# A two-layer attention and feed-forward block on one core: in the second attention layer the transpositions of q and k stand one step earlier

## The chip, the cores and the metric

The kernel runs on one core of a Trainium2 chip. The time is the device time of one execution of the whole program in microseconds (us); the median of several runs counts. The core has five engines that run their own instruction streams and wait for one another through semaphores: TensorE (PE, matmuls; PEld is its weight load), VectorE (DVE), ScalarE (ACT), GpSimd (POOL) and SyncE (SP), which only issues DMAs here.

## The reference

The input x is 2 x 512 tokens of 512 numbers in fp32. Four sublayers follow one another, each as x + layernorm(sublayer(layernorm(x))): a causal attention with rotary positions and grouped heads, a linear layer with LoRA, a second attention, and a SwiGLU feed-forward with LoRA. The change touches the second attention alone:

```python
q = (hidden_states @ Wq + bq).reshape(b, n, H, HD)      # H = 32 heads of HD = 128
k = (hidden_states @ Wk + bk).reshape(b, n, H, HD)
v = (hidden_states @ Wv + bv).reshape(b, n, H, HD)
q = rmsnorm(q, gq)
k = rmsnorm(k, gk)
scores = jnp.einsum('bnhd,bmhd->bhnm', q, k) * scale
attn = jax.nn.softmax(scores.astype(jnp.float32), axis=-1).astype(q.dtype)
out = jnp.einsum('bhnm,bmhd->bnhd', attn, v).reshape(b, n, H * HD)
return out @ Wo + bo
```

## The kernel before

Every fp32 product is made of three matmuls of halves (`product`, L83 to L85): hi x lo, lo x hi, hi x hi. Whatever enters a product is therefore split in two: ACT copies it into the rounded `_hi`, and DVE or POOL makes the remainder `_lo`.

The second attention is `paired_attention`. Its 32 heads are worked in NG = 8 groups of 4; group 0 and group 7 are written out, groups 1 to 6 are the six rounds of a hardware loop (`passes`, L252). A group has 8 **slots**, each one head of one of the two sequences, and 32 **steps** n = 0 to 31, four to a slot: step 4s + t makes the scores of slot s for 128 queries t against all 512 keys. Two slots of the same sequence form a pair (r, b). On each step every engine runs the same scheme for its own part:

- PE: the scores of step n (`l_score`, three matmuls of 128x512), and behind them what the table `USES1` has due at n: for a pair four tiles `y` (q and k of two heads for 128 tokens, 12 matmuls), two `v` (24 matmuls of 128x256), and for each slot one transposition of q (`tq`, four 128x128 transpositions at L485), one of k (`tk`), and the product of probabilities and v (`pv`, 12 matmuls that take the four chunks k = 0 to 3 of the transposed probabilities in turn). Output products (`l_out`) stand last in a step.
- DVE: negated row maximum of step n (`tops`, L675), the block transposition of the probabilities of step n - 1 (`turn_blocks`, L690), and then, one step behind PE, what empties the banks that PE filled: `l_y` (L639), `l_qT_lo` (L90), `l_kT_lo` (L646), `l_v_lo` (L90), `l_scaled` (L652, after `pv`). `l_probsT_lo` of the odd chunks and the additions to `acc` follow.
- ACT: exponentials of step n (L573), then, one step behind PE, `l_qT_hi` (L553), `l_kT_hi` (L555) or `l_v_hi` (L551), then `l_probsT_hi` (L579, two chunks at steps 4s + 8 and two at 4s + 9), squares of `y` for the RMS norm (L566), and the rounding of weights (L543).
- POOL: `l_probsT_lo` of the even chunks, the RMS norm (L748, L753), the remainders of weights (all L90).
- SP: the 16 DMAs that carry the block-transposed probabilities of a slot into `l_moved`, at step 4s + 4.

The table sets the order. An entry's number is the PE step, reckoned from the first step of the group; entries below zero belong to the group before. Inside one step the rank is y, v, tq, tk, pv. All uses share the four PSUM banks `general` in one ring: a use waits until the use four places ahead of it has been emptied (`n = m.done(USES1, x, d) - len(general)`, L459). `Pass.turns` gives each engine its due entries, DVE and ACT with a lag of one.

The waits around the change: the first scores of a slot wait until DVE has emptied the bank of `tk`, that is for `l_kT_lo` (L521), and all scores wait for the exponentials two steps back (L522). A `tq` of a pair's first slot waits for the pair's normed `y` (`s_yn`, L482). DVE writes a pair's first `y` only once the `tk` that still reads the old `y` is done.

```python
USES1 = {("y", r, b, t): 16 * r + 8 * b + n for r, b in PAIRS for t, n in enumerate((-15, -13, -12, -11))}
USES1 |= {("v", r, b, u): 16 * r + 8 * b + 7 + u for r, b in PAIRS for u in range(2)}
```

Of the kernel before, what the change touches and what calls it, by code (L numbers as in the profile page):

```python
# [33 lines left out]
SLOTS = GH * B  # L34
# [225 lines left out]
TURN_AT, MOVE_AT, LAND_AT, PV_AT, REST_AT = 1, 4, 8, 10, 12  # L260
# [12 lines left out]
PAIRS = [(r, b) for r in range(2) for b in range(B)]  # L273
USES1 = {("y", r, b, t): 16 * r + 8 * b + n for r, b in PAIRS for t, n in enumerate((-15, -13, -12, -11))}
USES1 |= {("v", r, b, u): 16 * r + 8 * b + 7 + u for r, b in PAIRS for u in range(2)}
USES1 |= {(kind, s): 4 * s + n for kind, n in (("tq", -3), ("tk", -2), ("pv", PV_AT)) for s in range(SLOTS)}
USES1 = Plan(USES1, lambda x: ("y", "v", "tq", "tk", "pv").index(x[0]))
OUTS1 = Plan({(r, b, t): 16 * r + 8 * b + 17 + t // 2 for r, b in PAIRS for t in range(TB)}, lambda x: x)
LOADS1 = {("wqk", r, c): 16 * r - 22 + c for r in range(2) for c in range(C)}
# [1697 lines left out]
```

How the kernel before makes its waits and increments, by code:

```python
def wait_past(engine, sem, m, per, count):  # L60
    if m.first and not (isinstance(count, int) and count > 0):
        return
    engine.wait_ge(sem, m.i * per + count)
# [70 lines left out]
    def spread(self, dve, *tiles):  # L135
        for r, t in tiles:
            dve.wait_ge(self.measured[r], 3 * t + 1)
            dve.bn_aggr(self.mean_var[:, r, t], self.stats[:, r, t]).then_inc(self.measured[r], 1)
        for r, t in tiles:
            dve.wait_ge(self.measured[r], 3 * t + 2)
            dve.tensor_scalar(self.var[:, r, t:t + 1], self.mean_var[:, r, t, 1:2], LN_EPS, None, ALU.add)\
                .then_inc(self.measured[r], 1)
# [1 line left out]
    def root(self, pool, r, t):  # L145
        pool.wait_ge(self.measured[r], 3 * t + 3)
        pool.tensor_tensor(self.rstd[:, r, t:t + 1], self.var[:, r, t:t + 1], self.half[:, 0:1], ALU.pow)\
            .then_inc(self.rooted[r], 1)
# [1 line left out]
    def center(self, dve, r, t):  # L151
        dve.wait_ge(self.rooted[r], t + 1)
        dve.scalar_tensor_tensor(self.bias[:, r, t:t + 1], self.mean_var[:, r, t, 0:1], -1.0,
                                 self.rstd[:, r, t:t + 1], ALU.mult, ALU.mult).then_inc(self.biased[r], 1)
# [1 line left out]
    def scaled(self, act, r, t, out, rows):  # L157
        act.wait_ge(self.biased[r], t + 1)
        act.activation(out, rows, ACT.Identity, bias=self.bias[:, r, t:t + 1], scale=self.rstd[:, r, t:t + 1])\
            .then_inc(self.normed[r], 1)
# [812 lines left out]
        @block.tensor  # L974
# [37 lines left out]
            for t in range(TT):
                pe.wait_ge(norms.normed[0], t + 1)
                if t >= 2:
```

## Time and profile before

| | us |
|---|---|
| median of 3 runs | 2364.04 (2362.09 to 2365.25) |
| the profiled execution, its own time | 2368.55 |
| its span, first to last instruction | 2366.8 |
| PE busy | 2132.5 (90%) |
| DVE busy | 1659.9 (70%) |
| ACT busy | 1296.0 (55%) |
| POOL busy | 1197.0 (51%) |

All views below are of this profiled execution. The second attention runs from 896 to 2109 us of the span. A view by instruction shows the start, the duration, the engine, the line, and the tiles as out<-in; the bracket is the idle time of the engine just before, and what ended it.

### The profile page before, as it was taken

The page shows a single profiled execution, that of the slowest core. Times are in us where ns is not written, and L with a number is a line of the kernel's source. Part 1 is how long each engine was busy: PE and PEld are TensorE (multiplying, and loading weights), DVE is VectorE, ACT ScalarE, POOL GpSimd, SP SyncE. Part 2 cuts the span into 40 slices and gives each one's busy share as a digit, 9 for nine tenths or more (in the row PEclk, how much of TensorE's full clock was granted, in tenths as well). Part 3 has the DMA queues.
Part 4 walks back from the last instruction along what each step waited for, and adds up shares of the span by engine and source line. Part 5 has one row for each costly group of instructions (what it writes and reads, how often), then busy time and mean ns, then how long its engine had stood idle before and what let it go on. Part 6 is the DMA issues. An engine that isn't in the chain of part 4 may idle for free. (4 is left out here: it accounts for less than half of the span.)

```text
span 2366.8 us, 38519 instructions
## 1 busy us (share of the span) xinstructions
PE 2132.5 (90%) x10535; PEld 1774.2 (75%) x10535; DVE 1659.9 (70%) x3013; ACT 1296.0 (55%) x3541; POOL 1197.0 (51%) x960
## 2 busy tenths in 40 slices
PE   4899999999999546999999999999999999756998
PEld 3688788888878435788878888788888888645887
DVE  3777777777778552777877878777778887754422
ACT  3666666666665343665655656656656566424321
POOL 4776766777664244544545445455454553324310
PEclk9999999999999777999999999999999999976999
DMA  2444343434434211444434344344444343333210
GB/s 72 109 111 112 107 114 106 118 94 115 119 85 118 88 62 33 115 113 108 105 89 117 103 111 106 91 113 107 111 107 105 93 112 89 94 116 99 77 45 27
DMA packets 165877, 231.51 MB, mean 98 GB/s; under 512 B 47281, under 2 KB 77137, under 8 KB 165745
## 3 DMA queue, kind: packets, MB, share of 16 engines
q1 hardware_dynamic: 165744, 229.97, 36.2%
q8 instruction: 56, 0.92, 0.2%
q14 instruction: 77, 0.62, 0.1%
HBM read 114.23 MB, written 6.55 MB: 51 GB/s over the span
## 5 line engine op out<-in xcount | busy, mean ns | idle before, releaser
L90 POOL TENSOR_TENSOR l_probsT_lo<-l_moved,l_probsT_hi 128x512 fp32r<-128x512 f32 (+2 forms) x256 | 289.6, 1136 | 274.0 <-ACT l_probsT_hi L579 247.1
L573 ACT ACTIVATE l_probs<-l_score,l_negtop 128x512 f32<-128x512 f32 x256 | 175.1, 684 | 342.8 <-DVE l_negtop L675 332.2
L90 DVE TENSOR_TENSOR l_probsT_lo<-l_moved,l_probsT_hi 128x512 fp32r<-128x512 f32 (+1 forms) x256 | 282.1, 1102 | 53.8 <-ACT l_probsT_hi L579 49.3
L1105 ACT ACTIVATE l_probs<-l_score,l_negtop 128x128 f32<-128x128 f32 (+3 forms) x256 | 134.9, 527 | 252.2 <-DVE l_negtop L1198 250.4
L83 PE MATMUL l_score<-l_kT_lo,l_qT_hi 128*128 128x512 f32 (+3 forms) x512 | 192.2, 375 | 55.8 <-DVE l_kT_lo L646 31.5
L83 PE MATMUL l_general<-l_w_qk_lo,xT_hi 128*128 128x512 f32 x512 | 201.7, 394 | 27.9 <-POOL l_w_qk_lo L90 27.9
L83 PE MATMUL l_out<-l_w_out_lo,l_oT_hi 128*128 128x512 f32 x512 | 209.2, 409 | 3.8 <-DVE l_oT_lo L701 2.8
L83 PE MATMUL l_general<-l_probsT_lo,l_v_hi 128*128 128x512 f32 (+3 forms) x512 | 189.2, 369 | 23.7 <-POOL l_probsT_lo L90 11.7
L675 DVE TENSOR_REDUCE l_negtop<-l_score 128x1 f32<-128x512 f32 x256 | 175.1, 684 | 40.4 <-PE l_score L85 37.5
L84 PE MATMUL l_general<-l_w_qk_hi,xT_lo 128*128 128x512 f32 x512 | 201.1, 393 | 0.0
L85 PE MATMUL l_general<-l_w_qk_hi,xT_hi 128*128 128x512 f32 x512 | 201.1, 393 | 0.0
L85 PE MATMUL l_out<-l_w_out_hi,l_oT_hi 128*128 128x512 f32 x512 | 201.0, 393 | 0.0
L84 PE MATMUL l_out<-l_w_out_hi,l_oT_lo 128*128 128x512 f32 x512 | 201.0, 393 | 0.0
L1198 DVE CUSTOM_DVE_ANT_0 l_score<-l_score,l_mask 128x128 f32<-128x128 f32 (+3 forms) x256 | 126.2, 493 | 88.4 <-PE l_score L85 88.0
L85 PE MATMUL l_general<-l_probsT_hi,l_v_hi 128*128 128x512 f32 (+3 forms) x512 | 184.9, 361 | 0.0
L84 PE MATMUL l_general<-l_probsT_hi,l_v_lo 128*128 128x512 f32 (+3 forms) x512 | 184.4, 360 | 0.0
L84 PE MATMUL l_score<-l_kT_hi,l_qT_lo 128*128 128x512 f32 (+3 forms) x512 | 184.1, 360 | 0.0
L85 PE MATMUL l_score<-l_kT_hi,l_qT_hi 128*128 128x512 f32 (+3 forms) x512 | 184.1, 360 | 0.0
L690 DVE STREAM_TRANSPOSE l_blocks<-l_probs 128x512 f32<-128x512 f32 x256 | 177.6, 694 | 0.2 <-ACT l_probs L573 0.2
L566 ACT ACTIVATE l_squares<-l_y 128x128 f32<-128x128 f32 x512 | 151.9, 298 | 40.2 <-DVE l_y L639 37.8
L83 PEld LDWEIGHTS l_score<-l_kT_lo,l_qT_hi 128*128 128x128 f32 x512 | 96.8, 189 | 101.2 <-issue 39.6
L90 POOL TENSOR_TENSOR l_w_qk_lo<-l_raw_qk,l_w_qk_hi 128x512 fp32r<-128x512 f32 x64 | 82.2, 1289 | 178.3 <-ACT l_w_qk_hi L543 178.3
(198 smaller groups left out, 6252.2 us busy)
## 6 DMA issues: line engine op xcount, KB each, us to landing
l_moved<-l_blocks SPq DMA_DIRECT2D x1024, 64.0 KB, 2.0
l_moved<-l_blocks SPq DMA_DIRECT2D x512, 80.0 KB, 2.1
l_inv_all<-inv_rows SPq DMA_DIRECT2D x32, 512.0 KB, 4.2
l_raw_out<-l_wo SPq DMA_DIRECT2D x64, 256.0 KB, 4.1
l_inv_all<-inv_rows SPq DMA_DIRECT2D x64, 256.0 KB, 3.6
ffn_w_lo_words<-f_w SPq DMA_DIRECT2D x33, 256.0 KB, 2.8
l_raw_q<-l_wq SPq DMA_DIRECT2D x32, 256.0 KB, 4.2
l_raw_qk<-l_wq SPq DMA_DIRECT2D x64, 128.0 KB, 2.9
```

The costliest lines, as they stand in the source:

```text
L83: nc.tensor.matmul(out, left.hi, right.lo, start=first, stop=False, skip_group_check=True)
L84: nc.tensor.matmul(out, left.lo, right.hi, start=False, stop=False, skip_group_check=True)
L85: return nc.tensor.matmul(out, left.hi, right.hi, start=False, stop=last, skip_group_check=True)
L90: return engine.tensor_tensor(out, full, hi.bitcast(F32), ALU.subtract)
L566: last = act.activation(squares[:, h], y[:, b, t, h * HD:(h + 1) * HD], ACT.Square, accum_out=sumsq[:, b, j:j + 1])
L573: act.activation(probs[:, n % NPR], score[n % 2][:], ACT.Exp, bias=negtop[:, n:n + 1], accum_out=total[:, n:n + 1]).then_inc(s_exp, 1)
L675: dve.tensor_reduce(negtop[:, n:n + 1], score[n % 2][:], AXX, ALU.max, negate=True)\
L690: dve.transpose(to, probs[:, n % NPR]).then_inc(s_block, 1)
L1105: act.activation(probs[:, n % NPR, 0:width[t]], score[n % 2][:, 0:width[t]], ACT.Exp, bias=negtop[:, n:n + 1], scale=-1.0, accum_out=total ...
L1198: dve.tensor_tensor_reduce(out=score[n % 2][:, 0:w], in0=score[n % 2][:, 0:w], in1=mask[:, S - w:S], scale=-SCALE, scalar=3.0e38, op0=ALU. ...
```

## The change

One tuple of `USES1` is altered. `tq` goes from step 4s - 3 to 4s - 4, and `tk` from 4s - 2 to 4s - 3. No instruction is added or taken away; the bank numbers follow the new order.

```diff
-USES1 |= {(kind, s): 4 * s + n for kind, n in (("tq", -3), ("tk", -2), ("pv", PV_AT)) for s in range(SLOTS)}
+USES1 |= {(kind, s): 4 * s + n for kind, n in (("tq", -4), ("tk", -3), ("pv", PV_AT)) for s in range(SLOTS)}
```

What this does to the order of work is seen at three places. The first is DVE in the loop body, steps 14 and 15, ahead of the scores of slot 4 (step 16); L675 opens a step. Before:

```order
1023 L675 TENSOR_REDUCE l1_negtop<-l1_score0 128x1
1024 L690 STREAM_TRANSPOSE l1_blocks<-l1_probs 128x4x4x32
1025 L630 REGISTER_ALU
1026 L639 TENSOR_TENSOR l1_y<-l1_general2,l1_b_qk 128x512
1027 L628 REGISTER_ALU
1028 L90 TENSOR_TENSOR l1_qT_lo<-l1_general3,l1_qT_hi 128x512
1029 L674 REGISTER_ALU
1030 L675 TENSOR_REDUCE l1_negtop<-l1_score1 128x1
1031 L690 STREAM_TRANSPOSE l1_blocks<-l1_probs 128x4x4x32
1032 L628 REGISTER_ALU
1033 L646 SCALAR_TENSOR_TENSOR l1_kT_lo<-l1_general0,l1_gains,l1_kT_hi 128x512
```

and now:

```order
1025 L675 TENSOR_REDUCE l1_negtop<-l1_score0 128x1
1026 L690 STREAM_TRANSPOSE l1_blocks<-l1_probs 128x4x4x32
1027 L630 REGISTER_ALU
1028 L639 TENSOR_TENSOR l1_y<-l1_general3,l1_b_qk 128x512
1029 L628 REGISTER_ALU
1030 L646 SCALAR_TENSOR_TENSOR l1_kT_lo<-l1_general0,l1_gains,l1_kT_hi 128x512
1031 L674 REGISTER_ALU
1032 L675 TENSOR_REDUCE l1_negtop<-l1_score1 128x1
1033 L690 STREAM_TRANSPOSE l1_blocks<-l1_probs 128x4x4x32
```

`l1_kT_lo` has moved from step 15, the last before the scores that need it, to step 14; `l1_qT_lo` has moved from step 14 to step 13.

The second is ACT in the loop body at step 13, where the chunks 2 and 3 of the transposed probabilities are rounded that `pv` takes at step 14; L573 opens the step. Before:

```order
682 L573 ACTIVATE l1_probs,l1_total<-l1_score1,l1_negtop 128x512
683 L579 ACTIVATE l1_probsT_hi<-l1_moved 128x4x128 x2
684 L559 REGISTER_ALU
685 L563 REGISTER_ALU
686 L566 ACTIVATE l1_squares,l1_sumsq<-l1_y 128x128 x4
```

and now:

```order
683 L573 ACTIVATE l1_probs,l1_total<-l1_score1,l1_negtop 128x512
684 L548 REGISTER_ALU
685 L553 ACTIVATE l1_qT_hi<-l1_general2 128x512
686 L579 ACTIVATE l1_probsT_hi<-l1_moved 128x4x128 x2
687 L559 REGISTER_ALU
688 L563 REGISTER_ALU
689 L566 ACTIVATE l1_squares,l1_sumsq<-l1_y 128x128 x4
```

`l1_qT_hi` now stands between the exponentials and `l1_probsT_hi`.

The third is PE in group 7, where no `y` stands between the uses: steps 21 and 22, up to the first chunk of `pv`. L485 are the transpositions. Before:

```order
3510 L83 MATMUL l1_score1<-l1_kT_lo,l1_qT_hi 128x512
3511 L84 MATMUL l1_score1<-l1_kT_hi,l1_qT_lo 128x512
3512 L85 MATMUL l1_score1<-l1_kT_hi,l1_qT_hi 128x512
3513 L485 MATMUL l1_general3<-ident,l1_y 128x128
3514 L485 MATMUL l1_general3<-ident,l1_y 128x128 x3
3515 L83 MATMUL l1_score0<-l1_kT_lo,l1_qT_hi 128x512
3516 L84 MATMUL l1_score0<-l1_kT_hi,l1_qT_lo 128x512
3517 L85 MATMUL l1_score0<-l1_kT_hi,l1_qT_hi 128x512
3518 L485 MATMUL l1_general0<-ident,l1_y 128x128
3519 L485 MATMUL l1_general0<-ident,l1_y 128x128 x3
3520 L83 MATMUL l1_general1<-l1_probsT_lo,l1_v_hi 128x512
```

and now:

```order
3510 L485 MATMUL l1_general3<-ident,l1_y 128x128
3511 L485 MATMUL l1_general3<-ident,l1_y 128x128 x3
3512 L83 MATMUL l1_score1<-l1_kT_lo,l1_qT_hi 128x512
3513 L84 MATMUL l1_score1<-l1_kT_hi,l1_qT_lo 128x512
3514 L85 MATMUL l1_score1<-l1_kT_hi,l1_qT_hi 128x512
3515 L485 MATMUL l1_general0<-ident,l1_y 128x128
3516 L485 MATMUL l1_general0<-ident,l1_y 128x128 x3
3517 L83 MATMUL l1_score0<-l1_kT_lo,l1_qT_hi 128x512
3518 L84 MATMUL l1_score0<-l1_kT_hi,l1_qT_lo 128x512
3519 L85 MATMUL l1_score0<-l1_kT_hi,l1_qT_hi 128x512
3520 L83 MATMUL l1_general1<-l1_probsT_lo,l1_v_hi 128x512
```

Both transpositions have passed one set of scores; `pv` follows its step's scores directly.

At the opening of the layer, which runs ahead of group 0, the order of PE's uses was y of pair (0,1) tiles 0 to 3, tq, tk. It is now y tiles 0 to 2, tq, y tile 3, tk.

## Rows read from the trace of the kernel before

**Rows 1.** The page: busy time, share of the span, instructions of each engine.

```profile
PE 2132.5 (90%) x10535; PEld 1774.2 (75%) x10535; DVE 1659.9 (70%) x3013; ACT 1296.0 (55%) x3541; POOL 1197.0 (51%) x960
```

**Rows 2.** Busy time by stretch: PE, PEld, DVE, ACT, POOL; then granted clock, DMA, GB/s.

```profile
1212.80:1216.20 3.40, 3.40 (x18) 3.40 (x17) 3.40 (x6) 2.30 (x5) 3.32 (x4) 0.50 0.19 41
1216.00:2026.00 810.00, 791.60 (x4107) 665.65 (x4105) 641.45 (x925) 482.00 (x1500) 401.21 (x286) 1.00 0.41 104
```

**Rows 3.** PE's waits from 896 to 2109: us in total, times, longest.

```profile
PE l_score L83 <- DVE l_kT_lo L646: 31.5, 59, 3.1
...
PE l_score L83 <- issue: 2.6, 1, 2.6
PE l_score L83 <- DVE l_scaled L652: 2.4, 1, 2.4
```

**Rows 4.** Instructions in order of time: the first scores of an odd slot.

```profile
1376.79 0.68 ACT L555 ACTIVATE l_kT_hi<-l_general,l_gains 128x512 fp32r<-128x512 f32 x1
...
1377.50 0.75 DVE L646 SCALAR_TENSOR_TENSOR l_kT_lo<-l_general,l_gains,l_kT_hi 128x512 fp32r<-128x512 f32 x1 [0.81 <-ACT l_kT_hi L555]
1377.67 0.39 PE L85 MATMUL l_general<-l_w_qk_hi,xT_hi 128*128 128x512 f32 x1
...
1378.38 0.49 PE L83 MATMUL l_score<-l_kT_lo,l_qT_hi 128*128 128x512 f32 x1 [0.32 <-DVE l_kT_lo L646]
...
1378.71 0.39 PE L84 MATMUL l_score<-l_kT_hi,l_qT_lo 128*128 128x512 f32 x1
```

**Rows 5.** The same wait at an ordinary turn of the loop, slot 0.

```profile
1648.77 0.49 PE L83 MATMUL l_score<-l_kT_lo,l_qT_hi 128*128 128x512 f32 x1 [0.71 <-DVE l_kT_lo L646]
```

**Rows 6.** Slot 0 at two turns of the loop.

```profile
1211.42 0.49 PE L83 MATMUL l_score<-l_kT_lo,l_qT_hi 128*128 128x512 f32 x1 [2.62 <-issue]
...
1501.42 0.75 DVE L646 SCALAR_TENSOR_TENSOR l_kT_lo<-l_general,l_gains,l_kT_hi 128x512 fp32r<-128x512 f32 x1 [1.19 <-ACT l_kT_hi L555]
...
1504.04 0.49 PE L83 MATMUL l_score<-l_kT_lo,l_qT_hi 128*128 128x512 f32 x1 [2.44 <-DVE l_scaled L652]
```

**Rows 7.** Steps 13 and 14 of a loop round: chunks 2 and 3 of slot 1.

```profile
1421.45 1.14 ACT L579 ACTIVATE l_probsT_hi<-l_moved 128x512 fp32r<-128x512 f32 x2
...
1422.21 1.28 POOL L90 TENSOR_TENSOR l_probsT_lo<-l_moved,l_probsT_hi 128x512 fp32r<-128x512 f32 x1
...
1422.36 0.60 PE L485 MATMUL l_general<-ident,l_y 128*128 128x128 f32 x4
...
1422.62 1.43 DVE L90 TENSOR_TENSOR l_probsT_lo<-l_moved,l_probsT_hi 128x512 fp32r<-128x512 f32 x1 [0.81 <-ACT l_probsT_hi L579]
...
1424.19 0.39 PE L83 MATMUL l_general<-l_probsT_lo,l_v_hi 128*128 128x512 f32 x1
...
1424.88 0.39 PE L83 MATMUL l_general<-l_probsT_lo,l_v_hi 128*128 128x512 f32 x1
```

**Rows 8.** Chunk 2 of slot 0 in the same round.

```profile
1403.20 1.75 POOL L90 TENSOR_TENSOR l_probsT_lo<-l_moved,l_probsT_hi 128x512 fp32r<-128x512 f32 x1
...
1406.32 0.39 PE L83 MATMUL l_general<-l_probsT_lo,l_v_hi 128*128 128x512 f32 x1
```

**Rows 9.** The opening: norm of pair (0,0), y tile 2 emptied, transpositions, first scores.

```profile
915.56 4.04 POOL L753 TENSOR_TENSOR l_y<-l_y,l_meansq 128x512 f32<-128x512 f32 x4
...
918.38 0.69 DVE L639 TENSOR_TENSOR l_y<-l_general,l_b_qk 128x512 f32<-128x512 f32 x1 [2.03 <-PE l_general L85]
...
925.08 0.50 PE L83 MATMUL l_score<-l_kT_lo,l_qT_hi 128*128 128x512 f32 x1 [3.14 <-DVE l_kT_lo L646]
```

**Rows 10.** Group 7, steps 19 and 20, on DVE and PE.

```profile
2026.86 0.70 DVE L690 STREAM_TRANSPOSE l_blocks<-l_probs 128x512 f32<-128x512 f32 x1
...
2029.03 1.06 DVE L652 TENSOR_TENSOR l_scaled<-l_general,l_inv_all 128x512 f32<-128x512 f32 x1
2029.17 0.80 PE L83 MATMUL l_score<-l_kT_lo,l_qT_hi 128*128 128x512 f32 x1 [2.96 <-DVE l_kT_lo L646]
...
2030.86 0.69 DVE L675 TENSOR_REDUCE l_negtop<-l_score 128x1 f32<-128x512 f32 x1 [0.77 <-PE l_score L85]
```

## The prediction

> **What bounds the kernel now.** The page says that PE is busy 90% of the span and the other engines 51 to 70% [rows 1]. That is a mean over all layers, so the next view is the busy time of the stretch that the change touches: from 1216 to 2026 us of the second attention PE is busy 791.6 of 810.0 us, at the full clock (granted 1.00, the 2.4 GHz level), DVE 79%, ACT 60%, POOL 50% [rows 2]. PE is the bound there, and a step can be gained only where PE stands still. The list of PE's waits says where: the largest is `l_score` at L83 on DVE's `l_kT_lo`, 31.5 us in 59 waits; two more of the same place are put down to other names, 2.6 and 2.4 us [rows 3]. They are two first scores of a group at a turn of the loop [rows 6]. That makes 36.5 us in 61 waits, close to one for each of the 64 slots: nearly every slot begins with PE waiting for k.
>
> The instructions in time order show why. At step 4s - 1 ACT does its exponentials, then `l_kT_hi` (1376.79 to 1377.47), then DVE makes `l_kT_lo` (1377.50 to 1378.25, after 0.81 us idle), and 0.13 us after its end the scores start [rows 4]. PE had been done 0.32 us earlier. The chain hangs on the exponentials of the step just before, not on the transposition, which PE made a step ahead.
>
> **Part 1: the wait goes.** `l_kT_lo` moves one step ahead on DVE and `l_kT_hi` on ACT, 3.5 us and more before the scores; the wait is at most 0.7 us at ordinary places [rows 5]. What does one wait cost in full? Normally a matmul of this shape starts 0.23 us after the one before (two chunks of `pv`, three matmuls apart, start 0.69 apart [rows 7]). The last matmul ahead of the scores starts at 1377.67, the scores at 1378.38: 0.71 us, of which 0.23 is normal, so 0.48 where 0.32 is booked as idle; and from there to L84 it takes 0.33, 0.10 more than normal [rows 4]. Each wait costs its idle time and 0.26 us. Over 61 waits: 36.5 + 61 x 0.26 = 52.4 us.
>
> **What of it stays.** (a) The first wait of the layer, 3.14 us [rows 9], hangs on its own transposition and has no step to hide behind: 3.4 with the 0.26. (b) The two turns of the loop with 2.62 and 2.44 us. At the second `l_kT_lo` ended at 1502.17 and the scores began at 1504.04, 1.87 later where 0.13 is usual [rows 4, 6]: something else was late by 1.7, and by 1.9 at the other (2.62 less the 0.71 of an ordinary turn [rows 5, 6]). I keep both: 3.6. (c) The opening. PE now wants `tq` after y tile 2, which it had finished by 918.38, but the norm of that pair ends at 915.56 + 4.04 = 919.60 [rows 9]: 1.3 us of new waiting, which POOL passes on to the next weights. The wait of slot 1, 2.0 us in the sum, is eaten by that 1.3 and by weights that come no sooner: 2.0. (d) In group 7 PE has little else to do, and DVE's chain counts. At step 20 the scores waited 2.96 us and the maxima began at 2030.86; without `l_kT_lo` DVE would go from the transposition (ends 2027.56) to `l_scaled` (1.06) and be at the maxima by 2028.6 [rows 10]. Of 3.2 us (with the 0.26) 2.2 are won and 1.0 stays; slot 7, at step 28, has the same order of work and I take the same: 2.0. The sum is 52.4 - 3.4 - 3.6 - 2.0 - 2.0 = **41.4 us**.
>
> **Part 2: what is moved past what.** No instruction is added. ACT does `l_qT_hi` at steps 4s - 3, just ahead of `l_probsT_hi` of chunks 2 and 3, and DVE `l_qT_lo` ahead of `l_probsT_lo` of chunk 3; `pv` of the slot before wants these one PE step on. This is the place where a new wait could arise. In a loop round, slot 1: POOL ends chunk 2 at 1423.49 and PE takes it at 1424.19, 0.70 later; DVE ends chunk 3 at 1424.05 and PE takes it at 1424.88, 0.83 later [rows 7]. Slot 0 has 1.37 [rows 8]. PE's `pv` comes sooner by one block of transpositions, 0.60 at most [rows 7]. ACT's `l_qT_hi` has no row of its own; the nearest is `l_kT_hi`, 0.68, and for `l_qT_lo` it is `l_kT_lo`, 0.75 [rows 4]. From above: all in series, chunk 3 comes 0.68 + 0.75 + 0.13 later and is wanted 0.60 sooner, 2.2 less the 0.83 is 1.3 us in slots 1 and 5, 16 times: 21 us. From below nothing, since both engines also lose work ahead of it: at the end of the step before the slot DVE drops 0.81 of waiting and 0.75 of `l_kT_lo`, so `l_scaled` and all behind it run up to 1.5 us sooner, and PE only 0.5. I take nothing, nearer the lower end, because steps 4s to 4s + 2 form one chain on ACT and DVE, and that chain starts sooner by more than is put into it.
>
> The ring of four banks: at steps 1 and 5 of 8 `tk` now comes one use nearer to its predecessor, but the use four ahead was emptied by DVE in the step before, and a whole `y` (12 x 0.23 = 2.7 us on PE) stands between. Nothing. POOL and SP keep their order. The exponentials that the scores wait for lie two steps back, and their order is not touched.
>
> The order of ports. DVE's chunk 3 takes 1.43 us while POOL is at work beside it [rows 7]. The Trainium skill (SBUF — State Buffer, Who interferes with whom) says that a DVE instruction with two SBUF inputs and a GpSimd instruction that reads SBUF shut each other out for a whole instruction; by it a chunk 3 that slips behind POOL's next instruction would wait for all of it. With 1.3 us for that, 16 times, its sum would be as high as the 21 us above; the rows agree that the two stretch when side by side, and do not show which slips.
>
> The turns of the loop. Of six, two show an extra 1.7 to 1.9 us [rows 6] and one ordinary one shows 0.71 [rows 5]. It may be that something at every turn takes up to 0.71 and now lies under the wait for k; bound 0 to 4 x 0.71 = 2.8 us. I take 0. The Trainium skill (Runtime: NRT & Kernel Launch, Instruction fetch mechanics) says that a taken branch whose target is not in the two pages held forces a fetch before the engine goes on; by it all turns would pay, and the sum would be 38.5.
>
> The clock. After the 2.62 us of idle the granted clock was 0.50 (1.2 GHz) from 1212.8 to 1216.2 [rows 2, 6]. If it stays full there, some 1.5 us more are won; not in the sum.
>
> **The time.** The profiled execution took 2368.55 us, 4.5 over the median of 2364.04; 41.4 off it would leave 2327.2, and off the median 2322.6. I forecast **2323**.
>
> **Rivals.** *A: the probabilities come late.* ACT and DVE don't make up for the moved pair, and chunks 2 and 3 bind in slots 1 and 5: 41 - 21 = 20 us won, 2344 at the worst, about 2340 with part of it. For it: the smallest margins of the layer, 0.70 and 0.83. Against it: the head start of 1.5 us.
> *B: slower.* The same place, but the shift grows along the chain, since DVE is 79% busy and its instructions stretch beside POOL. Per group the change wins about 5.1 us. If all eight `pv` come late by L against today's order, the loss per group is 2 (L - 0.70) + 6 (L - 1.37), which passes 5.1 at L = 1.84 us. At L = 2.2 it is 8.0, 2.9 a group more than is won, 8 groups: 23 us slower, 2387. For it: the moved pair together is 1.56 and the 0.60 of PE make 2.2. Against it: that takes everything in series and no head start anywhere.
> *C: a wait takes its place.* The scores start no sooner, since `tk` waits for its bank or `l_kT_lo` sits behind other work on DVE: 2364. Against it: `l_kT_lo` would have to come later by a whole step, 3.5 us.
> *D: more.* The two long turns and the clock go as well: 41.4 + 3.6 + 1.5 = 46.5, 2317.5; with small gains 2314.
>
> **How the numbers follow.** The forecast with its small terms (2314 to 2331) gets 0.74, D lies in it; A 0.16; C 0.05; B 0.05. The range must leave out no more than 0.2: from 2314 to 2342 it holds the forecast and most of A. A measurement of this kernel tells 0.2%, 4.7 us, from no change. Faster by more: 0.74 + 0.16 and nothing of C, 0.90; same 0.05; slower 0.05.
>
> **What would show it.** In the profile after: PE's waits of `l_score` on `l_kT_lo` gone but for the first, some 3 to 5 us left in all; PE busy over 99% from 1216 to about 1990; the layer shorter by about 41 us, each group of the loop by 5; `l_score` starting 3 us after `l_kT_lo` ends; about 1.3 us of PE idle before `tq` at 918. A shows as PE waits of `l_general` L83 on `l_probsT_lo`, 16 of about 1 us; B as the same in all slots; C as waits of `l_score` or L485 on DVE. Wrong would be the step that says ACT and DVE start sooner than they are loaded, or that the first scores wait for k alone.

## The result and the profile after

The changed kernel took 2334.53 us (median of 4 runs, 2332.97 to 2336.80) against 2363.51 us for the kernel before (4 runs, 2362.09 to 2365.25). The ratio is 0.9873, with a 95% interval of 0.9861 to 0.9886: faster by 29.0 us. The forecast was 2323, 41.4 us less, in a range from 2314 to 2342. The sign and the range held; of the forecast gain, 0.70 came. The profiled execution took 2333.02 us (span 2331.2) against 2368.55 us (span 2366.8), so the two traces differ by 35.6 us in the span.

The page's first line, which answers to [rows 1], and PE's waits from 896 to 2109 us, which answer to [rows 3] (us in total, times, longest):

```profile
PE 2118.4 (91%) x10535; PEld 1776.9 (76%) x10535; DVE 1643.7 (71%) x3013; ACT 1294.0 (56%) x3541; POOL 1181.9 (51%) x960
```

```profile
PE l_score L83 <- issue: 8.5, 5, 2.2
...
PE l_score L83 <- ACT l_probs L573: 4.0, 4, 1.3
PE l_score L83 <- DVE l_kT_lo L646: 3.1, 1, 3.1
...
PE l_general L485 <- POOL l_y L753: 1.4, 1, 1.4
```

Sixty of the 61 waits for k are gone; the one left is the first of the layer, 3.1 us. What is new is the first row: five waits of the first scores, 8.5 us in all, with nothing that the profile shows as their releaser ("issue"). The row on ACT belongs to the last group, that on POOL to the opening. The dots leave out other rows, among them PE's waits in `pv` for `l_probsT_lo`: 9.0 us in 5, all in and behind the last group, where the kernel before had 11.7 us in 6.

The first scores of an odd slot in the changed kernel, in order of time, as in [rows 4]:

```profile
1357.79 0.68 ACT L555 ACTIVATE l_kT_hi<-l_general,l_gains 128x512 fp32r<-128x512 f32 x1
...
1358.50 0.75 DVE L646 SCALAR_TENSOR_TENSOR l_kT_lo<-l_general,l_gains,l_kT_hi 128x512 fp32r<-128x512 f32 x1 [0.23 <-ACT l_kT_hi L555]
...
1365.02 0.39 PE L83 MATMUL l_score<-l_kT_lo,l_qT_hi 128*128 128x512 f32 x1
```

k is ready at 1359.25 and wanted at 1365.02, 5.77 us later; the scores carry no idle time. In even slots inside a round the margin is 2.7 us.

PE busy by stretch, at and behind the first turn of the loop, as in [rows 2] (us, busy of PE, PEld, DVE, ACT, POOL, granted clock, DMA, GB/s):

```profile
1201.30:1204.70 3.40, 3.40 (x13) 3.11 (x14) 1.73 (x4) 0.93 (x3) 3.32 (x4) 0.50 0.03 7
1205.00:1990.00 785.00, 778.25 (x4098) 665.32 (x4097) 629.44 (x923) 481.34 (x1501) 389.20 (x285) 1.00 0.42 107
```

PE is busy 99.1% of the loop's stretch. Of the 6.75 us that are left, 6.38 stand at the four turns of the loop in this stretch. One of them, with the last matmul ahead of it:

```profile
1342.32 0.28 PE L85 MATMUL l_general<-l_w_v_hi,xT_hi 128*128 128x256 f32 x1
...
1344.28 0.49 PE L83 MATMUL l_score<-l_kT_lo,l_qT_hi 128*128 128x512 f32 x1 [1.68 <-issue]
```

All five turns look like this, at 1201.28, 1344.28, 1486.19, 1627.44 and 1769.25 us, with 2.16, 1.68, 1.64, 1.41 and 1.65 us of idle PE. In the kernel before two of five were long [rows 6] and an ordinary one had 0.71 us, which was the wait for k [rows 5]. (Groups 1 to 6 are the loop, so it turns back five times; the "six" of the prediction was one too many.)

The span by stage, from the starts of PE's instructions at each border, in us. The forecast column is the prediction's own sum, cut at the same borders (idle time for k there, 0.26 more for each wait, less what was to stay):

| stage | before | after | gained | forecast |
|---|---|---|---|---|
| first y tile to the first scores, and group 0 | 168.5 | 162.9 | 5.6 | 4.5 |
| groups 1 to 6, the loop | 873.3 | 849.8 | 23.5 | 30.5 |
| group 7 to the last scores | 133.9 | 127.6 | 6.3 | 6.4 |
| end of the layer | 36.9 | 36.1 | 0.8 | 0 |
| sum | 1212.6 | 1176.4 | 36.2 | 41.4 |

The loop falls short by 7.0 us; the rest comes out 1.8 us above its forecast.

### The profile page after: what moved, and what is told of

Its sections match the earlier page's. It is cut to its first block and busy times, and to the rows that moved or that the text cites. A ratio compares the mean times of both kernels' runs of the same rounds, so it can differ in the third digit from the quotient of the medians.

```text
span 2331.2 us, 38519 instructions
## 1 busy us (share of the span) xinstructions
PE 2118.4 (91%) x10535; PEld 1776.9 (76%) x10535; DVE 1643.7 (71%) x3013; ACT 1294.0 (56%) x3541; POOL 1181.9 (51%) x960
## 5 line engine op out<-in xcount | busy, mean ns | idle before, releaser
L90 POOL TENSOR_TENSOR l_probsT_lo<-l_moved,l_probsT_hi 128x512 fp32r<-128x512 f32 (+2 forms) x256 | 272.1, 1068 | 309.8 <-ACT l_probsT_hi L579 282.8
L573 ACT ACTIVATE l_probs<-l_score,l_negtop 128x512 f32<-128x512 f32 x256 | 175.7, 686 | 381.2 <-DVE l_negtop L675 381.0
L675 DVE TENSOR_REDUCE l_negtop<-l_score 128x1 f32<-128x512 f32 x256 | 175.8, 687 | 99.7 <-PE l_score L85 97.6
L579 ACT ACTIVATE l_probsT_hi<-l_moved 128x512 fp32r<-128x512 f32 x256 | 147.1, 629 | 0.0
```

The lines of the kernel that those rows point to most:

```text
L90: return engine.tensor_tensor(out, full, hi.bitcast(F32), ALU.subtract)
L573: act.activation(probs[:, n % NPR], score[n % 2][:], ACT.Exp, bias=negtop[:, n:n + 1], accum_out=total[:, n:n + 1]).then_inc(s_exp, 1)
L579: act.activation(probsT_hi[:, :, k], moved[:, slot % 2, :, k], ACT.Copy).then_inc(s_land_hi, 1)
L675: dve.tensor_reduce(negtop[:, n:n + 1], score[n % 2][:], AXX, ALU.max, negate=True)\
```

## What the experiments asked

Two questions. Is it the place of k alone that makes the gain? And why are all five turns slow now, which the prediction had bounded at 2.8 us and set to nothing? The page of each kernel has a row on the instruction fetches: queue, packets, MB, share of the engines. That of the kernel before, and then that of the changed one:

```profile
q8 instruction: 56, 0.92, 0.2%
```

```profile
q8 instruction: 83, 1.36, 0.3%
```

Each of these packets has 16,384 bytes. In the compiled program an instruction of PE takes 64, so a packet carries 256; the run with 256 empty instructions below fetches just one packet more. PE's program in the changed kernel has 9,789 instructions, 38.2 packets. The body of the loop has 1,592 of them in both kernels, 4785 to 6376 counted from 0 (the traces record 1,590 in a round). Counted from the start of the program, it begins at instruction 178 of a packet and ends at 233 of the sixth packet after it, so it touches seven.

In the trace of the kernel before, no packet is fetched in the rounds that follow a quick turn, and nine in each of the two that follow a slow one; in the changed kernel nine are fetched in each of the five rounds (38 + 2 x 9 = 56, 38 + 5 x 9 = 83; a round is counted here from 2 us ahead of the branch that leads into it). The packets' times tie them to the stops. In the changed kernel the branch that ends a round is executed at 1196.92, 1340.40, 1482.35, 1623.83 and 1765.39 us. Each time one fetch starts 0.8 to 1.0 us ahead of it and another 1.0 us behind it, which takes 0.9 to 1.5 us, and then the first scores start. Both slow turns of the kernel before have the fetch 1.0 us behind the branch too; its three quick turns have none within 10 us.

All experiments are compared with runs of the kernel before that were taken beside them; its medians there were 2364.7, 2365.1 and 2366.0 us. The changed kernel itself was not run again beside them: its 2334.5 us is that of the first comparison.

## Experiments on the turns of the loop

**Written out.** The loop over groups becomes straight code, in both kernels.

```diff
+def written_out(engine, body, end):
+    for i in range(NG):
+        body(Pass(i, i == 0, i == NG - 1, end))
...
-            passes(pe, body, END1)
+            written_out(pe, body, END1)
```

(the same on SP, ACT, DVE and POOL)

> The changed kernel with the eight groups of the second attention written out, so that there is no loop and no turn in it. Theory 1 and theory 2 both: no idle at slot 0 of groups 2 to 6, 2334 less 10 to 12 = about 2323 us, if bringing in code in a row costs nothing, as groups 0 and 7 suggest. If code that comes in a row does cost, stalls appear in the middle of groups, and the time is not under 2330.

> The kernel before with the eight groups written out. The wait for k stays at every slot (0.17 to 0.71 us idle each); 2363.5 less 0 to 4 = about 2361 us. Against after_written_out it gives what the change is worth where no loop is in play: 38 to 42 us by the sum of the waits; 29 if the shortfall lies in the waits themselves and not in the turns.

The changed kernel written out took 2320.34 us (2318.45 to 2321.21), ratio 0.9811 [0.9795, 0.9827]; the kernel before written out 2359.96 us (2358.5 to 2360.94), ratio 0.9976 [0.9967, 0.9986]. Without turns the change is worth 39.6 us, within 2 us of the forecast 41.4 and inside the 38 to 42 that were expected. PE in the changed kernel written out, from 1210 to 1980:

```profile
1210.00:1980.00 770.00, 770.00 (x4061) 659.25 (x4060) 624.98 (x917) 476.54 (x1495) 383.00 (x282) 1.00 0.42 109
```

PE is never idle there, though 32 packets are fetched in this stretch (67 in the whole program). A fetch in straight code costs nothing that can be seen; a fetch at a turn does.

**Shift by 80.** The loop stays, and 80 empty instructions go ahead of PE's part of the layer, in both kernels.

```diff
+            for _ in range(80):
+                pe.wait_ge(s_const, 64)
+                pe.nop(nofuse=True)
             for x in USES1.early:
                 bank_use(x, start, 0)
```

> The changed kernel with 80 more instructions on PE, waits on a semaphore that has long reached its value, at the opening of the second attention, where PE is idle for some 19 us anyway. They shift PE's loop body by 80 places (from 4785 to 6376 of PE's instructions to 4865 to 6456) and change nothing else. Theory 1 (the 1.4 to 2.2 us of idle at each of the five turns of the loop come from PE's code having to be brought in again, and whether it has to depends on where the body lies and how far the fetching runs past its end): the shift changes how many turns are slow; if the body then stays held, the five idle stretches go and the instruction packets fall from 83 to about 55, 2334 less about 12 = 2322 us. Theory 2 (the idle at the turns is the price of a taken branch, or comes from the semaphores there): five stretches of 1.4 to 2.2 us as before the shift, 2334 us.

> The kernel before with the same 80 instructions. Theory 1: no slow turn is left (its profile had two), and the 2.62 and 2.44 us become 0.7, the wait for k alone; the median, 2363.5, falls by 0 to 4, and every run lies within 1 us of the others. With after_shift80 it gives the change without the turns: the difference is 38 to 42 us. Theory 2: same as the kernel before, 2363.5, difference to the changed one 29.

The changed kernel: 2324.40 us (2321.96 to 2325.23), ratio 0.9825 [0.9809, 0.9842]. No turn is slow, each round takes 139.55 us, and the page counts 38 packets, with none in the rounds behind a turn. The kernel before: 2367.05 us (2364.84 to 2368.66), ratio 1.0009 [0.9999, 1.0019]. The expectation of a fall was a miss in the time, though not in the turns: its rounds fell from 873.3 to 868.3 us together, and all are alike at 144.7. The empty instructions only ran once the constants had landed, and the first y tile started at 899.6 instead of 896.2; the last group took 136.1 instead of 133.9 us, with 15.8 instead of 10.2 us at half clock. Against the shift by 50 below, this one is 3.9 us longer in the changed kernel and 2.3 us in the kernel before. The difference between the two kernels shifted by 80 is 42.7 us, where 38 to 42 were expected. The next ones wait for an earlier load (`s_b[0]`).

**Shift by 50,** with this earlier wait.

```diff
+            for _ in range(50):
+                pe.wait_ge(s_b[0], 32)
+                pe.nop(nofuse=True)
```

> The changed kernel with 50 empty instructions on PE ahead of the layer, run while PE has nothing to do. In the changed kernel the loop body is PE's instructions 4785 to 6376, 64 bytes each, fetched in packets of 16,384 bytes (256 instructions): it ends 232 instructions into a packet. 80 empty ones put the end 56 into the next packet and the slow turns were gone. Theory: what counts is how near to the end of a packet the body ends and how many packets it touches (7 there). With 50 it ends 26 into an eighth packet: five slow turns stay, over 80 fetched packets, 2331 to 2338. Rival: any shift, or the delay of the start, frees the turns: no slow turn, some 38 packets, 2319 to 2325.

> The kernel before with the same 50 empty instructions. Unshifted it has two slow turns of five and 56 fetched packets, with 80 none and 38. Theory of the packets: the body now touches eight, and all five turns are slow here too, over 80 packets, 1.7 us more at three further turns: 2366 to 2372. Rival, that the slow turns come from how far PE's sequencer runs ahead and not from the place: no change or fewer slow turns, 2358 to 2365.

My theory of the number of packets fell. The body touched eight packets, and yet the turns were quick: the changed kernel took 2320.47 us (2318.41 to 2323.67), ratio 0.9816 [0.9799, 0.9832], the kernel before 2364.76 us (2362.43 to 2367.99), ratio 0.9999 [0.9989, 1.0009]. The changed kernel's fetches, and its loop:

```profile
q8 instruction: 38, 0.62, 0.1%
```

```profile
1206.00:1980.00 774.00, 773.25 (x4075) 661.69 (x4074) 626.66 (x925) 479.56 (x1497) 382.96 (x282) 1.00 0.43 108
```

38 packets for the whole program, and none in the loop. Its rounds take 837.3 us together, where the changed kernel as it stands takes 849.8: 12.5 us for five turns, of which 8.5 are idle time of the first scores; the rest lies behind them. Between the two shifted kernels lie 44.3 us, more than forecast. Most of the 4.7 us over the written-out pair lie in the kernel before: the six rounds of the changed one take 837.3 us either way, while those of the kernel before take 868.3 us shifted and 864.7 written out, with waits for k of 3.0 us in a round against 2.3. So the worth of the change without slow turns depends on the form of the kernel before, 39.6 to 44.3 us.

**Shifts by 20 and 256** (the same edit with other counts) should tell "any shift" from "the place in the packet".

> The changed kernel with 20 empty instructions on PE ahead of the layer. Shifts of 50 and 80 both took the slow turns away, so the count of packets that the body touches (eight with 50, seven with 80) is not it. Two theories are left. P, the place in the packet: slow when the body ends shortly ahead of a packet's end, at instruction 233 of 256 in the unshifted kernel; with 20 it ends at 253, nearer still, and the five slow turns stay: 141 to 142 us a round, over 40 packets of PE's instructions behind 890 us in place of 18, 2331 to 2337. Q, any shift frees them, or the empty instructions themselves: 139.55 us in every round, some 18 packets, 2318 to 2324.

> The same with 256 empty instructions, just one packet of 16,384 bytes: every instruction of the loop stands at the same place in its packet as in the changed kernel. They take PE past the time at which the weights are ready, so the layer starts later, by up to 20 us, which is to be left out; what counts are the rounds. P, the place in the packet: slow turns as without a shift, rounds of 141 to 142 us and an idle stretch of 1.4 to 2.2 us before the first scores of each round. Q, any shift frees them: 139.55 us in every round.

With 20 the time was 2342.07 us, with 256 it was 2349.64 us (one run each). The first scores behind the first turn, with 20:

```profile
1200.14 0.75 PE L83 MATMUL l_score<-l_kT_lo,l_qT_hi 128*128 128x512 f32 x1 [2.12 <-issue]
```

and with 256:

```profile
1217.43 0.49 PE L83 MATMUL l_score<-l_kT_lo,l_qT_hi 128*128 128x512 f32 x1 [1.59 <-issue]
```

Both have five slow turns, 83 and 84 packets, and 857.9 and 850.1 us for the six rounds, against 849.8 unshifted and 837.3 with 50 or 80. With 256 the layer starts 17 us later (913.5 us), which accounts for its time against the unshifted kernel's, 15.1 us more; the place in the packet is the old one, and so are the turns. "Any shift frees them" is refuted, and so is "the empty instructions do it". In the changed kernel the turns go with the place of the body in the packets: slow in three placements, where it ends at instruction 233 (0 and 256) or 253 (20) of 256, quick in two, where it ends at 27 or 57. The body's length is the same in all, so its start moves with its end, and these runs can't tell which of the two counts. With 20 the turns have 9.7 us of idle time in five, and the loop 13.7 us at half clock where the changed kernel has 3.4.

Why that is so was not shown. What the traces show is that all the slow turns have a fetch that starts 0.9 to 1.9 us behind the branch, the quick ones of all kernels have none there, and a slow round fetches nine packets where the body touches seven. It would fit that the fetcher, ahead of the branch, already asks for the packet behind the body, and that the first packet of the body is given up for it; nothing in the trace says which packet is dropped. The counts would fit if eight packets were held and 29 to 58 instructions stood ahead of the program in its first packet: then the slow bodies touch eight packets, nine with the one behind them, and the quick bodies seven, eight with it. That is worked out from the five placements alone, and no run tests it. By itself a fetch ahead of the branch doesn't make a turn slow: the first turn with the shift by 50 has one, 2.3 us ahead of the branch, and PE isn't idle there. The place alone doesn't decide either: the kernel before, at the same place, has slow turns in two of five, and why is not shown.

## Experiments on the change itself

The lines of `USES1` below are shown against the kernel before.

**Only k** (`tk` at 4s - 3, `tq` stays at 4s - 3).

```diff
-... (("tq", -3), ("tk", -2), ("pv", PV_AT)) ...
+... (("tq", -3), ("tk", -3), ("pv", PV_AT)) ...
```

> Only the transposition of k stands a step earlier (both at step 4s - 3); that of q stays where it was before. If the first scores wait for l_kT_lo alone, as the prediction says, the wait goes as in the changed kernel: PE's waits of l_score on l_kT_lo a few us in all, an ordinary round of the loop 139.5 us instead of 144.7, and the time 2325 to 2338, by how many turns of the loop are slow (2 to 3.4 us each). Rival: q and k made in the same step queue up on ACT and DVE, l_kT_lo comes late again by part of a step, and moving q as well was needed: 2345 to 2360, with waits on l_qT_lo or l_kT_lo left.

2329.32 us (2326.18 to 2331.72), ratio 0.9852 [0.9835, 0.9868]. PE's waits:

```profile
PE l_score L83 <- issue: 8.3, 5, 1.8
...
PE l_score L83 <- DVE l_kT_lo L646: 3.1, 1, 3.1
```

The same picture as with both moved: 60 waits gone, five slow turns. The time is no worse without the move of q: 5.2 us less than the changed kernel, whose four runs (2332.97 to 2336.80, taken at another time) all lie above these. The last of the six rounds, with no turn behind it, takes 139.45 us against 139.95 in the changed kernel, all six 845.6 against 849.8, and the 1.4 us on POOL's norm in the opening is not there.

**Only q** (`tq` at 4s - 4, `tk` stays at 4s - 2).

```diff
-... (("tq", -3), ("tk", -2), ("pv", PV_AT)) ...
+... (("tq", -4), ("tk", -2), ("pv", PV_AT)) ...
```

> Only the transposition of q stands a step earlier (step 4s - 4); that of k stays at 4s - 2. My theory: q was never late, the wait of the first scores for l_kT_lo stays, 55 to 61 waits with 30 us and more, an ordinary round 144 to 145 us and the time 2358 to 2366. Rival: with l_qT off ACT's and DVE's way the step before the scores is lighter and l_kT_lo comes sooner by up to 0.7 us a slot: 2330 to 2345.

```profile
PE l_score L83 <- DVE l_kT_lo L646: 39.9, 60, 3.1
```

2378.47 us (2376.08 to 2378.89), ratio 1.0054 [1.0037, 1.0071]: slower by 13 us, which neither theory had. The waits for k all stay: 39.9 us in 60, where the kernel before has 36.5 in 61 under three names [rows 3]. The page counts 83 packets in place of 56, and all five turns are slow (8.7 us of idle time in five, booked on k, against 7.2). The first round, with no slow turn in it, has 3.8 us of waits against 2.9, so the ordinary ones grow too. By the traces the six rounds took 878.0 instead of 873.3 us, and about 1 us each was lost ahead of the layer (which the change doesn't touch), in the opening, group 0, group 7 and the end. The two spans lie 9.6 us apart and the medians 13; the rest is not explained.

**A better opening.** In the changed kernel the transpositions of slot 0 run at 919.28 (q) and 922.49 (k), with a y tile between, and the scores wait 3.08 us. Here k of slot 0 stands right behind q. The kernel is shifted by 50, so that no turn is slow.

```diff
+USES1[("tk", 0)] = -4
```

> The changed kernel shifted by 50 (2320.5 us), and slot 0's transposition of k stands at step -4, right behind that of q and ahead of y tile 3 of the next pair of heads. In the profile of the changed kernel tq ran at 919.28 us, then y tile 3, then tk at 922.49, and the scores 3.67 us behind it, 3.08 of them idle. Now tk should run at about 919.65 and y tile 3 (2.8 us) lie in the idle time, so that the first scores start up to 2.8 us sooner. My expectation: the wait of l_score on l_kT_lo falls from 3.1 to under 1 us, and the time by 1 to 3 us, to 2317.5 to 2319.5, unless the next weights (ready no sooner) eat it, then no change: 2320.5.

2321.43 us (2317.91 to 2322.29), ratio 0.9812 [0.9796, 0.9829], no gain over the 2320.47 of the shifted kernel. PE in the opening, in order of time:

```profile
917.22 1.07 PE L486 MATMUL l_general<-ident,l_y 128*128 128x128 f32 x8 [1.40 <-POOL l_y L757]
...
920.89 0.39 PE L83 MATMUL l_score<-l_kT_lo,l_qT_hi 128*128 128x512 f32 x1
```

The wait for k is gone, and the scores start 27.0 us after the first y tile instead of 29.3. But group 0 takes 136.8 instead of 133.0 us, because the next y tile waits for its weights that much longer:

```profile
935.63 0.77 PE L83 MATMUL l_general<-l_w_qk_lo,xT_hi 128*128 128x512 f32 x1 [12.76 <-POOL l_w_qk_lo L90]
```

In the changed kernel that wait has 9.36 us:

```profile
937.63 0.76 PE L83 MATMUL l_general<-l_w_qk_lo,xT_hi 128*128 128x512 f32 x1 [9.36 <-POOL l_w_qk_lo L90]
```

In both this tile starts 18.4 us after the first transposition of q (917.22 and 919.28): POOL's work sets it, and the first scores don't count.

**All together:** this opening, k and q both at 4s - 3 in the other slots, shifted by 50.

```diff
-... (("tq", -3), ("tk", -2), ("pv", PV_AT)) ...
+... (("tq", -3), ("tk", -3), ("pv", PV_AT)) ...
+USES1[("tq", 0)] = USES1[("tk", 0)] = -4
```

> As the run before it, but in the other slots q stays at step 4s - 3 beside k (q and k of slot 0 at -4). k alone gave the same ordinary round as the changed kernel, 139.45 against 139.55 us. Theory, that only k's place matters: within 1.5 us of the run before it, 0.6 us a layer less from the rounds and up to 2 us less in the last group (126.9 against 127.6 us there): 2316 to 2319. Rival: q beside k makes other steps late once the turns are quick: 2320 to 2325.

2318.64 us (2317.20 to 2320.33), ratio 0.9802 [0.9785, 0.9818], the lowest median of all, 15.9 us under the changed kernel and inside the 2316 to 2319 that were expected. Its interval overlaps those of the other kernels without slow turns, so its lead of 2 to 3 us is not shown by the times; its rounds take 139.19 us, against 139.58 in the run before it.

## Why the prediction was right, and where not

**The wait, Part 1: right.** The chain over the exponentials was the cause. k alone moves all of it and q alone none, as the steps said. The price of a wait, its idle time and 0.26 us, holds: an ordinary round fell from 144.73 to 139.55 us with either shift, 5.18 where "each group of the loop by 5" was forecast. Of these 3.03 were idle time of eight waits, so 0.27 a wait came on top. Over the six rounds it is 31.0 us (868.3 to 837.3), against 30.5 in the sum.

**(a) and (c), first wait and opening: right within 1.2 us.** The first wait stayed (3.1 us, 3.14 before [rows 9]). The new wait of `tq` on the norm is 1.40 us, forecast 1.3 (919.60 less 918.38 is 1.2 by its own rows), and the next weights came later, counted from the first y tile (41.1 instead of 39.7 us):

```profile
919.28 0.63 PE L485 MATMUL l_general<-ident,l_y 128*128 128x128 f32 x4 [1.40 <-POOL l_y L753]
```

**(d), group 7: right in its sum, in part by luck.** 6.3 us were gained, 6.4 forecast. The wait at step 20, 2.96 us [rows 10], is gone; the scores of the next two steps wait for the exponentials instead. The chain to the first of these waits, in order of time:

```profile
1993.18 1.28 DVE L708 TENSOR_TENSOR acc<-l_out,acc 128x512 f32<-128x512 f32 x2
1993.20 0.39 PE L83 MATMUL l_score<-l_kT_lo,l_qT_hi 128*128 128x512 f32 x1
...
1994.38 0.68 DVE L675 TENSOR_REDUCE l_negtop<-l_score 128x1 f32<-128x512 f32 x1
...
1995.09 0.69 ACT L573 ACTIVATE l_probs<-l_score,l_negtop 128x512 f32<-128x512 f32 x1 [2.61 <-DVE l_negtop L675]
...
1995.92 0.50 PE L83 MATMUL l_score<-l_kT_lo,l_qT_hi 128*128 128x512 f32 x1 [0.76 <-ACT l_probs L573]
```

PE waits for ACT's exponentials, and ACT had waited for DVE's maxima (1994.38 to 1995.06), which stood behind the additions to `acc`. So DVE's chain is the bound, as the step had it. Its size was not: there are four such waits with 4.0 us in all (1.5 at slot 5, 2.5 at slot 7), where the step left 2.0. PE's idle time from the start of group 7 to the last scores fell by only 4.1 us (12.7 to 8.6); the other 2.2 us of the 6.3 lie in time booked as busy, which was not traced further.

**Part 2, the moved pair: right.** Rival A had its smallest margins in chunks 2 and 3 of slots 1 and 5, 0.70 and 0.83 us [rows 7]. The same place in the changed kernel:

```profile
1407.24 1.29 POOL L90 TENSOR_TENSOR l_probsT_lo<-l_moved,l_probsT_hi 128x512 fp32r<-128x512 f32 x1 [0.45 <-ACT l_probsT_hi L579]
...
1407.71 1.37 DVE L90 TENSOR_TENSOR l_probsT_lo<-l_moved,l_probsT_hi 128x512 fp32r<-128x512 f32 x1 [0.35 <-ACT l_probsT_hi L579]
...
1409.70 0.39 PE L83 MATMUL l_general<-l_probsT_lo,l_v_hi 128*128 128x512 f32 x1
...
1410.39 0.39 PE L83 MATMUL l_general<-l_probsT_lo,l_v_hi 128*128 128x512 f32 x1
```

Chunk 2 ends at 1408.53 and is taken at 1409.70, 1.17 later; chunk 3 ends at 1409.08 and is taken at 1410.39, 1.31 later. The margins grew by 0.5 us, so the head start of ACT and DVE outweighed what was put into their chain. No wait of `pv` on these chunks stands in the loop. Rivals A and B are refuted, and C with them.

**(b) and "the turns of the loop": wrong.** The step was "bound 0 to 2.8 us. I take 0", beside "I keep both: 3.6". It asked whether something at each turn lay under the wait for k, and took the 0.71 of an ordinary turn as its ceiling. But a quick turn of the kernel before fetches nothing, and with the shifts by 50 and 80 the quick turns of the changed kernel have no idle time at all: nothing was hidden there. What happened is that quick turns became slow ones. A long turn was something that could befall any of the five, and the step had their price in hand: 1.7 to 1.9 us of idle time each [rows 6]. In the traces the changed kernel loses 12.5 us at its turns and the kernel before 5.0, so 7.5 us of the gain were given back, which is the shortfall of the loop in the table, 7.0, beside 0.5 that the waits brought over their sum. By the medians the shift by 50 is worth 14.1 us to the changed kernel (2334.5 to 2320.5) and 0.3 us to the kernel before. An upper end of five slow turns, 5 x 1.9 less the 3.6 that were kept, about 6 us, would have stood in the rows.

The Trainium skill (Runtime: NRT & Kernel Launch, Instruction fetch mechanics) was weighed there, with 38.5 us by its rule that a taken branch whose target isn't held makes the engine wait for a fetch. It pointed the right way for the changed kernel: all five turns pay, each with a fetch that starts 1.0 us behind the branch. The price put on it, 0.71 us at each of four turns, was the prediction's own, and too low. With the shifts by 50 and 80 no turn pays, although the body touches seven or eight packets, so for PE a window of two pages does not hold. The same section gives PE a memory of 128 KiB, 2,048 instructions, which is eight packets; with that the 38 packets of the shifted kernels agree. The slow rounds fetch nine, one more than that. The prediction had used the one sentence and not the other.

**The clock** stayed as it was: 3.4 us at 0.50 (1.2 GHz) behind the longest stop, 2.16 us at 1201.28, as before behind 2.62 [rows 2, 6]. Rival D, in which long turns and clock go as well, is what the shifted kernels show: 2320.5 us, D forecast 2317.5.

**The profiled execution.** The prediction took 41.4 off the median as if every run had the turns of the profiled one, 4.5 us above it. That the unshifted and the shifted kernel before have the same median, while the profiled trace loses 5.0 us at its turns, fits that most of its runs have fewer slow turns. That was not seen in a trace.

## What to carry to other kernels

A wait that stands at the head of nearly every slot is worth its idle time and the broken pipelining behind it, and it goes when its whole chain, not only its last producer, moves ahead of the slot; try first the one operand that is late, because moving the other along can cost. Where PE is busy 99%, look at the turns of the loop next: "issue" before the first matmul of a round, with a count of fetched instruction packets that grows with the rounds, means that the loop is fetched anew. Writing it out tells in one run what that costs. Empty instructions ahead of it tell it too, but only if their number is one that frees the turns: 50 and 80 did here, 20 and 256 did not. A rare long wait in one trace is not a constant of the kernel: bound it by all the places where it could stand.

## What was unexpected of the hardware

Whether a PE loop of 1,592 instructions is kept or fetched again in each round went with where it lies in the packets of 256: in the changed kernel kept with its end at instruction 27 or 57 (38 packets in the whole program), fetched with its end at 233 or 253 (83 and 84, nine in each round), at 1.4 to 2.5 us of idle PE in a turn. The place is not all of it: at 233, by the profiled executions, moving two transpositions in the order turned two slow turns of five into five. And straight code of the same work fetches 67 packets, with PE busy 770.00 of 770.00 us.
